# Two cross-attention blocks on one core: PSUM dealt out as four banks for scores and three single banks for raw products

## The reference

```python
scores = jnp.einsum('bhqd,bhkd->bhqk', Q, K) / math.sqrt(D_K)
time_bias = -0.1 * jnp.abs(t[None, :] - t[:, None])
attn = jax.nn.softmax(scores + time_bias[None, None], axis=-1)
out = jnp.einsum('bhqk,bhkd->bhqd', attn, V)
...
E = NORM * jnp.einsum('bqhd,bkhd->bhqk', qh, kh)
A = jax.nn.softmax(E, axis=-1)
out = jnp.einsum('bhqk,bkhd->bqhd', A, vh)
```

## Time and profile before

| | |
|---|---|
| median of 3 runs (lowest to highest) | 979.24 us (975.6 to 981.1) |
| profiled execution: its own time, its span | 982.73 us, 980.9 us |
| PE, DVE, ACT, POOL busy | 86%, 60%, 44%, 24% of the span |
| L1006, maxima over 128x1024 | 256 of 1220 ns, 299.8 us |
| L442, raw products | 512 of 514 ns, 169.1 us |
| L467, scores (ps_a, ps_misc) | 342 of 474 ns, 170 of 469 ns |
| L735, exponentials | 512 of 604 ns, 296.1 us |
| L479, weighings (two records each) | 1024 of 632 ns, 142.7 us |
| groups of layer 0, from one output copy (L727) to the next | 11.23 us |

### The profile page before, as it was taken

How to read it: one execution, slowest core, us unless ns; L and a number is a source line. 1 busy time by engine, 2 the same in 40 slices (tenths; PEclk the granted TensorE clock), 3 DMA queues, 4 the chain that set the end, 5 groups by cost and what they waited for, 6 DMA issues and landing times. The chain is left out here.

```text
span 980.9 us, 11821 instructions
## 1 busy us (share of the span) xinstructions
PE 844.2 (86%) x4356; PEld 507.4 (52%) x4356; DVE 584.0 (60%) x938; ACT 433.4 (44%) x813; POOL 240.2 (24%) x269
## 2 busy tenths in 40 slices
PE   2972899999989989953899998984799999999985
PEld 1630334444336669921344343432577877878765
DVE  1833988988715836725778887855841423345026
ACT  0130487887765366420478676775321021120110
POOL 1100255455532376500000000013122111121220
PEclk9995699999999999985589897998799998999997
DMA  9646122222005300045712121200000000000000
GB/s 225 187 137 196 48 79 72 68 66 79 22 3 170 87 1 1 1 135 168 263 50 77 51 74 49 67 2 0 2 1 1 1 1 22 1 20 3 0 22 22
DMA packets 39626, 60.67 MB, mean 62 GB/s; under 512 B 7112, under 2 KB 17096, under 8 KB 39312
## 3 DMA queue, kind: packets, MB, share of 16 engines
q1 hardware_dynamic: 38704, 58.99, 20.7%
q0 software_dynamic: 864, 0.92, 0.6%
HBM read 40.02 MB, written 18.87 MB: 60 GB/s over the span
## 5 line engine op out<-in xcount | busy, mean ns | idle before, releaser
L1006 DVE TENSOR_REDUCE row_max<-ps_wide 128x2 f32<-128x1024 f32 x256 | 299.8, 1220 | 37.6 <-PE ps_wide L442 37.6
L442 PE MATMUL ps_wide<-stack_k,stack_q 48*128 48x512 f32 x512 | 169.1, 514 | 60.4 <-DVE planes L981 45.5
L735 ACT ACTIVATE probs<-ps_a 128x512 f32<-128x512 f32 x342 | 193.4, 604 | 59.3 <-PE ps_a L467 57.7
L467 PE MATMUL ps_a<-stack_q,stack_k 62*128 62x512 f32 (+1 forms) x342 | 144.6, 474 | 6.0 <-ACT probs L735 3.9
L479 PE MATMUL ps_out<-probs,vals 128*32 128x512 f32 x1024 | 142.7, 632 | 2.9 <-POOL probs L873 0.5
L442 PEld LDWEIGHTS ps_wide<-stack_k,stack_q 48*128 48x128 f32 x512 | 72.8, 210 | 90.8 <-DVE planes L981 47.2
L827 ACT ACTIVATE hid_full<-ps_a 128x512 f32<-128x512 f32 x32 | 19.1, 598 | 217.5 <-PE ps_a L651 156.1
L735 ACT ACTIVATE probs<-ps_misc 128x512 f32<-128x512 f32 x170 | 102.7, 604 | 25.9 <-PE ps_misc L467 22.4
L467 PEld LDWEIGHTS ps_a<-stack_q,stack_k 62*128 62x128 f32 (+1 forms) x342 | 63.0, 198 | 97.4 <-ACT probs L735 65.9
L873 POOL TENSOR_TENSOR probs<-probs,fixes_sb 128x512 f32<-128x512 f32 x64 | 81.9, 1279 | 85.8 <-ACT probs L735 85.8
L929 POOL TENSOR_TENSOR hid_lo<-hid_full,hid_hi 128x512 fp32r<-128x512 f32 x32 | 42.6, 1332 | 194.6 <-ACT hid_hi L828 194.6
(11 more groups left out here) (140 smaller groups left out, 1219.1 us busy)
## 6 DMA issues: line engine op xcount, KB each, us to landing
planes_k<-planes SPq DMA_DIRECT2D x32, 256.0 KB, 3.7
planes_q<-planes SPq DMA_DIRECT2D x32, 256.0 KB, 4.1
stack_q<-planes_q SPq DMA_DIRECT2D x64, 128.0 KB, 2.8
stack_k<-planes_k SPq DMA_DIRECT2D x64, 128.0 KB, 2.8
stack_q<-planes_q SPq DMA_DIRECT2D x64, 64.0 KB, 2.7
stack_k<-planes_k SPq DMA_DIRECT2D x64, 64.0 KB, 2.5
w_e_raw<-in_L_W SPq DMA_DIRECT2D x1, 4096.0 KB, 12.9
ctxT<-in_ctxT SPq DMA_DIRECT2D x1, 2048.0 KB, 16.0
```

The costliest lines, as they stand in the source:

```text
L442: mm(raw_slot(("pair", g, p))[:, i * S:(i + 1) * S], stack_q[at, slot(g, c) + q * P:slot(g, c) + (q + 1) * P], stack_k[at, slot(g, c):slot ...
L467: mm(score_slot(("tile", n))[:], stack_k[at, slot(g, c) + k * P:slot(g, c) + (k + 1) * P], stack_q[at, slot(g, c):slot(g, c) + S], start=T ...
L735: do(probs[n % PROBS][:, j, :], score_slot(("tile", n * HG + j))[:], ACT.Exp, scale=0.25).then_inc(exp_done, 1)
L1006: v.tensor_reduce(row_max[:, g % 2, :, p], raw_slot(("pair", g, p))[:].rearrange("p (i k) -> p i k", i=2), AX, ALU.max).then_inc(max_done, 1)
```

## The change

PSUM is dealt out anew in the attention. Scores and turned maxima take four banks in turn: ps_a0, ps_a1, ps_misc and the second bank of ps_wide1. Raw products and turned outputs take three single banks in turn: the two of ps_wide0 and the first of ps_wide1. The item of the raw list is no longer a pair but a half, and each half waits for the maximum of the half three back. The maximum is one instruction per half, over 512 columns (now L1008), instead of one per pair over 1024; there are 512 instead of 256. PE's order of matmuls stays, but before group 0 the half i = 1 comes first in a pair, as it already did later.

```diff
--- before.py
+++ after.py
@@ -189,7 +189,8 @@
         pw = [ctx.enter_context(nc.psum_tensor(f"ps_wide{i}", [P, 2 * S], F32)) for i in range(2)]
         po = ctx.enter_context(nc.psum_tensor("ps_out", [P, S], F32))
         pm = ctx.enter_context(nc.psum_tensor("ps_misc", [P, S], F32))
-        tiles_x = (ps[0], ps[1], pm)
+        tiles_x = (ps[0][:], ps[1][:], pm[:], pw[1][:, S:2 * S])
+        tiles_m = (pw[0][:, 0:S], pw[0][:, S:2 * S], pw[1][:, 0:S])
 
         def wide(k):
 
@@ -230,7 +231,8 @@
                     if p == PAIRS // 2 and g >= BEHIND + 2:
                         yield ("out", g - BEHIND - 2)
                     if g < G:
-                        yield ("pair", g, p)
+                        yield ("half", g, p, 1)
+                        yield ("half", g, p, 0)
 
         def score_items():
 
@@ -247,11 +249,11 @@
 
         def raw_slot(item):
 
-            return pw[raw_at[item] % 2]
+            return tiles_m[raw_at[item] % 3]
 
         def score_slot(item):
 
-            return tiles_x[score_at[item] % 3]
+            return tiles_x[score_at[item] % 4]
 
         def vals_pair(i):
 
@@ -412,20 +414,20 @@
                 def raw_free(item):
 
                     m = raw_at[item]
-                    if m < 2:
+                    if m < 3:
                         return
-                    past = raws[m - 2]
-                    if past[0] == "pair":
-                        pe.wait_ge(max_done, past[1] * PAIRS + past[2] + 1)
+                    past = raws[m - 3]
+                    if past[0] == "half":
+                        pe.wait_ge(max_done, 2 * (past[1] * PAIRS + past[2]) + 2 - past[3])
                     else:
                         pe.wait_ge(normalised, past[1] + 1)
 
                 def score_free(item):
 
                     m = score_at[item]
-                    if m < 3:
+                    if m < 4:
                         return
-                    past = tiles_in[m - 3]
+                    past = tiles_in[m - 4]
                     if past[0] == "tile":
                         pe.wait_ge(exp_done, past[1] + 1)
                     else:
@@ -436,10 +438,9 @@
                     c, q = divmod(p, QT)
                     if p == 0 and first:
                         pe.wait_ge(sem(f"stack_loaded{l}_{g % RING}"), 16 * LOADS * (g // RING + 1))
-                    if first:
-                        raw_free(("pair", g, p))
+                    raw_free(("half", g, p, i))
                     at = slice(HALF * i, HALF * i + KS)
-                    mm(raw_slot(("pair", g, p))[:, i * S:(i + 1) * S], stack_q[at, slot(g, c) + q * P:slot(g, c) + (q + 1) * P],
+                    mm(raw_slot(("half", g, p, i)), stack_q[at, slot(g, c) + q * P:slot(g, c) + (q + 1) * P],
                        stack_k[at, slot(g, c):slot(g, c) + S], start=True, stop=True).then_inc(raw_done, 1)
 
                 def turn_maximum(g):
@@ -464,7 +465,7 @@
                     n = (g * QT + k) * HG + 2 * c + i
                     score_free(("tile", n))
                     at = slice(HALF * i, HALF * i + rows)
-                    mm(score_slot(("tile", n))[:], stack_k[at, slot(g, c) + k * P:slot(g, c) + (k + 1) * P],
+                    mm(score_slot(("tile", n)), stack_k[at, slot(g, c) + k * P:slot(g, c) + (k + 1) * P],
                        stack_q[at, slot(g, c):slot(g, c) + S], start=True, stop=True).then_inc(scores_done, 1)
 
                 def weigh(n):
@@ -483,8 +484,8 @@
                     for p in range(PAIRS):
                         if g == 1 and p == PAIRS // 2:
                             turn_maximum(0)
-                        for i in range(2):
-                            for_maximum(g, p, i, i == 0)
+                        for i in (1, 0):
+                            for_maximum(g, p, i, i == 1)
                 pe.wait_ge(sem(f"rows_in{l}"), 16 * (N_ATT if l == 0 else 2))
                 pe.wait_ge(sem(f"vals_read{l}"), T // 2)
                 for g in range(G):
@@ -732,7 +733,7 @@
                     act.wait_ge(scores_done, n * HG + j + 1)
                     if j == 0 and n >= PROBS:
                         act.wait_ge(pv_done, HG * (n - PROBS + 1))
-                    do(probs[n % PROBS][:, j, :], score_slot(("tile", n * HG + j))[:], ACT.Exp, scale=0.25).then_inc(exp_done, 1)
+                    do(probs[n % PROBS][:, j, :], score_slot(("tile", n * HG + j)), ACT.Exp, scale=0.25).then_inc(exp_done, 1)
 
                 keep_maximum(0)
                 planes_left(act, l, 2 * B * C)
@@ -855,7 +856,7 @@
                 def split_maximum(g):
 
                     max_neg_ready, max_high = sem(f"max_neg{l}"), sem(f"max_high{l}")
-                    pool.wait_ge(sem(f"max_done{l}"), PAIRS * (g + 1))
+                    pool.wait_ge(sem(f"max_done{l}"), 2 * PAIRS * (g + 1))
                     wait(pool, sem(f"max_split{l}"), g)
                     v.tensor_scalar(max_neg[:], row_max[:, g % 2], -1.0, None, ALU.mult).then_inc(max_neg_ready, 1)
                     pool.wait_ge(max_neg_ready, g + 1)
@@ -1000,11 +1001,12 @@
 
                 def maximum(g, p):
 
-                    dve.wait_ge(sem(f"raw_done{l}"), 2 * (g * PAIRS + p + 1))
-                    if p == 0:
-                        wait(dve, sem(f"max_neg{l}"), g - 1)
-                    v.tensor_reduce(row_max[:, g % 2, :, p], raw_slot(("pair", g, p))[:].rearrange("p (i k) -> p i k", i=2),
-                                    AX, ALU.max).then_inc(max_done, 1)
+                    for i in (1, 0):
+                        dve.wait_ge(sem(f"raw_done{l}"), 2 * (g * PAIRS + p) + 2 - i)
+                        if p == 0 and i == 1:
+                            wait(dve, sem(f"max_neg{l}"), g - 1)
+                        v.tensor_reduce(row_max[:, g % 2, i, p:p + 1], raw_slot(("half", g, p, i)), AX, ALU.max
+                                        ).then_inc(max_done, 1)
 
                 def normalise(g):
```

## The result

The changed kernel takes 991.0 us (median of 4 runs, 989.1 to 994.9) against 979.0 before: a ratio of 1.013, with an interval of 1.009 to 1.018. The profiled execution took 994.88 with a span of 993.0; it lies 3.9 above its median, as the one before (982.73) lay 3.7 above its own, so the difference of the spans, 12.1, can be taken apart line by line.

A forecast was written before the change was run, and what follows sets the result against it. It took a 2.60 us loop, score, exponential, freed score bank, weighing, next score, to bound the kernel. Layer 0 +4.7 and layer 1 +5.7 made +10.4 on the median 979.2: 989.6 us, range 984 to 995.

The forecast's parts named there:

- The step: Ordinary key step with raw products: its fourth raw matmul waits for the first one's maximum; 2.70 us instead of 2.60.
- m: Time of one maximum over 512 columns on VectorE, taken as 0.69 us.
- The turning step: Key step in which maxima and outputs are turned: the next step's first score comes 0.21 us later.
- S3 without a wait: Key step's last score matmul no longer waits for an exponential; could run about 0.8 us after the first score, not 1.18.
- The opening: Maxima ahead of and around group 0 of each layer: 1.5 us later in layer 0, 0.9 in layer 1.
- The variance in layer 1: After groups 7 and 11, VectorE's 3.6 us of other work stalls PE a step earlier: 1.3 us more each.
- The last two groups: Without raw products, four score banks break the exponential's loop: 2.03 us a step, 0.58 less; 3.5 gained per layer.
- The clock rival: Groups with raw products: the clock falls, a step then costing 4.07 us instead of 2.60; about 1007 us; chance 0.08.
- The early-start rival: Ordinary steps bound by VectorE's four maxima, 2.46 us, if the fourth raw matmul isn't late; about 959 us; chance 0.07.

The follow-up runs named there:

- three score banks: Kernel after the change with three banks for scores instead of four, its three single raw banks kept: 997.31 us, ratio 1.020 to the kernel before.
- late banks: Kernel before, scores given five banks from each layer's last two groups on: 974.26 us; second kernel, also with the variance work split over groups: 962.2 us.
- four single raw banks: Kernel after the change with four single banks for raw products and three for scores, maxima still over 512 columns: 980.97 us, ratio 1.004.
- C's maximum short: Kernel after the change with the third maximum of each key step over 256 of its 512 columns: 984.16 us, ratio 1.006.
- A's short: Kernel after the change with the first maximum of each key step over 256 of its 512 columns: 957.86 us, ratio 0.979.
- its twin with three score banks: Kernel after the change with each key step's first maximum over 256 columns and three banks for scores instead of four: 979.33 us, ratio 1.003.

## Why the prediction was right, and where it wasn't

The forecast was 989.6 against 991.0, by the mechanism that happened. Its terms against the profiled executions:

- *The step.* Predicted 2.70, measured 2.74. The size of m was right: 0.683 against 0.69, and VectorE's pitch 0.604 against 0.605. What was small by 0.03 is the start: VectorE took A up 0.07 after A's end, not 0.04; the other 0.01 lies between PV and S0. The turning step grew by 0.15, not 0.21: A's maximum began 1.39 after its start (212.47 against 211.08), not 1.43, and the next S0 came 1.00 after PV, not 1.02. A group: 0.55 against the forecast 0.51, 6.47 in twelve groups of layer 0 against 12 x 0.51 = 6.1.
- *S3 without a wait.* Right; the run with three score banks showed that this wait was not just hidden but worth nothing there.
- *The opening.* Predicted 1.5 in layer 0; the maxima took 24.24 for 40 against 22.72 for 20, +1.52. The first copy came 3.83 later. From the first maximum to the first copy it is 35.13 before, 39.06 after, and 37.09 with three score banks, with the same maxima ahead of it. So about 2.0 goes with the change (the 1.52 and some 0.4 for the steps behind it), and about 1.9 with this one execution, in which the clock stood at half for longer: from 70 us to the first copy its mean was 0.58 before, 0.55 after, and 0.59 with three score banks. In layer 1 (predicted 0.9) the first maximum stood 0.1 less behind the last copy of layer 0 than before, and the way from there to the first copy took 1.38 more; together they are the 1.27 between the layers' attention. The two kernels with late banks have the code of before on that way and took 0.9 and 0.6 less than before, so chance could make up much of the 1.38. The windows from 70 us to the first copy of layer 0, after and with three score banks:

```profile
70.00:130.45 60.45, 39.09 (x121) 17.35 (x121) 36.00 (x59) 15.57 (x31) 9.64 (x15) 0.55 0.38 114
```
```profile
70.00:126.22 56.22, 36.44 (x121) 16.72 (x121) 36.01 (x59) 15.47 (x32) 9.65 (x15) 0.59 0.39 118
```

- *After attention.* +2.66 in the profiled execution, at a mean clock of 0.91 against 0.92, with the same instructions. The forecast had nothing here. With three score banks the same code took 309.32, against 309.19 before, and with four single raw banks 309.1. But where the last groups are shorter it took 311.85 after, 310.6 with C's maximum short and 311.1 and 312.4 with late banks; with A's short it was 305.4, against 306.4 for its twin with three score banks. One profiled execution of each doesn't tell whether an earlier end of attention brings this on or chance does; it stays open.
- *The variance in layer 1.* This step failed. I took 1.3 more for each of two stalls and argued from PE's stall at D and the clock's fall behind it. Beyond their own group's length, the stalls cost 4.4 and 4.7 in the kernel after, 5.6 and 5.9 with three score banks, 6.5 and 5.7 with C short: 5.5 in the mean. With double banks they cost 5.1 and 6.6 in the kernel before, 4.4 and 6.4 with the late banks: 5.6. (The other runs fit: 4.5 twice with A short, 6.5 twice with that and three score banks, 6.0 and 6.1 with four single raw banks.) That PE stalls one matmul pair earlier makes no difference that these show. What varies with the cost is the time at half clock: over the twelve groups the mean clock was 0.98 after, where the two stalls cost 9.2 together, 0.96 with three score banks, where they cost 11.5, and 0.94 with C short, where they cost 12.1. In the two compared here they happened to cost 9.2 after against 11.7 before, so the twelve groups of layer 1 grew by 3.9, where the forecast's steps and stalls came to 8.3.
- *The last two groups.* Predicted -3.5 a layer. The stretches give -2.67 and -3.35, but they begin with a piece that has raw products and costs about 0.3; the bank by itself gave 2.97 and 3.59, as taking it away showed. Two steps took 4.08 against the forecast 4.06.
- *The clock rival.* In twelve groups PE was called busy 127.41 of 141.23, 90%, with the granted clock at 1.00 throughout. The fall didn't come.

The terms corrected: the steady one was 1.0 too small (24 groups x 0.04), the last groups 0.4 too optimistic (7.0 against 6.6), the variance 2.6 too large; and with the variance gone, the four ordinary and two turning steps that the sum had left out around it come back in, 4 x 0.14 + 2 x 0.15 = 0.9. That makes 10.4 + 1.0 + 0.4 - 2.6 + 0.9 = 10.1. The difference of the spans without what differs only between executions (1.9 in the opening, -2.5 at the stalls) and without the 2.7 after attention is 12.1 - 2.1 = 10.0. The rest between that and the medians' 12.0 lies within the interval of 1.009 to 1.018, and so does the 12.7 with the 2.7 in it. That the forecast came within 1.4 us of the median is in part luck: its errors in the stalls and in the steps cancel, and the terms for the openings and the stalls are no larger than the differences between executions.

The early-start rival named the right place: the gain needs A's maximum early enough that D isn't late. With A's maximum short the step fell to 2.48 and the kernel to 2.1% below before. Only the kernel's real maximum can't be that short.

## What to carry to other kernels

When a pool of banks is dealt anew, write down for each taker whose bank it gets and how old that user is, and add up the loop through it; the bank gained counts only if the bank lost doesn't close a loop that is as long. To see whether an engine's load or one instruction's place binds, cut the same amount from two of its instructions in turn and compare. Use spare banks in the stages where they are spare, and cut long side work on a feeding engine into pieces that its idle time over the next steps takes up (here 0.4 to 0.5 each, with 0.24 idle in an ordinary step).

## What the runs showed of the hardware

A maximum over 512 columns from PSUM took 0.683 us by its own record and 0.604 from one to the next back to back. The Trainium skill, in "VectorE: DVE Perf Modes", section "The TRN2 errata — SBUF-src ops pay a fixed extra latency per instruction", would have its own time at 0.66 (an estimate from the price that the prediction quotes); the trace has 0.02 more.

TensorE's granted clock stayed at its upper level (1.00, 2.4 GHz) with steps in which it waited 0.34 at the same place every 2.74 us, at 90% busy, as it had at 83% in the last groups before; in layer 1's groups it fell to the lower (1.2 GHz) only behind single long stops. The first matmul after such a stop in layer 1, with 3.63 idle ahead of it, and the four microseconds that follow, at a mean of 0.57:

```profile
561.64 0.50 PE L443 MATMUL ps_wide<-stack_k,stack_q 48*128 48x512 f32 x1 [3.63 <-DVE row_max L1008]
```
```profile
562.00:566.00 4.00, 4.00 (x21) 1.24 (x20) 2.58 (x5) 1.83 (x4) 0.00 (x0) 0.57 0.10 33
```

PE is called busy in all of these four. The rule in "TensorE: Matmul & The Clock Gate" of the Trainium skill, section "A second HAM failure mode: psum-queue depth-cycling", would have falls with small waits as well; no run here shows them in these stretches.

How long the half clock lasts after the same event differs between executions. Behind the same two stops of layer 1 the mean clock of the twelve groups was 0.98 in the kernel after and 0.96 with three score banks, and the stops cost 9.2 and 11.5 us. A difference of 2 to 3 us in a single stretch has to be set against this before it is put down to an edit.
